# Gate and up products of the last layer by seven block products in place of eight

## What is computed

```
g = jnp.einsum('bsh,ehf->ebsf', x, w_gate)      # h = 256, f = 1024, 8 experts
u = jnp.einsum('bsh,ehf->ebsf', x, w_up)
h = jax.nn.silu(g) * u
expert_out = jnp.einsum('ebsf,efh->ebsh', h, w_down)
cw = router_probs * gate_weights                # two softmaxes over the 8 experts
cw = cw / (jnp.sum(cw, axis=-1, keepdims=True) + 1e-09)
out = jnp.einsum('ebsh,bse->bsh', expert_out, cw)
```

## Time and profile before

| | |
|---|---|
| three runs, median | 1771.9 us |
| profiled execution, span from the first to the last instruction | 1770.5 us |
| PE busy, of the span | 93% |
| first gate or up matmul of the last layer | 701.3 us |
| last matmul | 1765.2 us |
| clock granted to PE, 750 to 1650 us | 1.00 of full speed |
| DVE, ACT, POOL busy in 880 to 1010 us (one expert is 130.6 us) | 70.1, 24.4, 15.2 us of 130 |

### The profile page before, as it was taken

The page is one execution under the profiler, slowest core; times in us unless marked ns, Lnnn a source line. Parts: engine busy times, 40 slices in busy tenths (PEclk is TensorE's granted clock), DMA queues, the critical chain, the costliest instruction groups (busy, mean ns, idle before and its releaser), DMA issues.

```text
span 1770.5 us, 24802 instructions
## 1 busy us (share of the span) xinstructions
PE 1646.7 (93%) x8306; PEld 1355.8 (77%) x8306; DVE 1043.8 (59%) x2102; ACT 478.5 (27%) x845; POOL 459.8 (26%) x297
## 2 busy tenths in 40 slices
PE   6999987689966888999999999999999999999998
PEld 5896663388864777788888888888888888888887
DVE  6666778556656786554555554554655544645654
ACT  4455332134332455312212212212112112112111
POOL 2552257688526612100201201101101102102000
PEclk9998998899987998899999999999999999999999
DMA  6994022278643201000200200200101101101001
GB/s 204 265 315 185 24 71 87 84 242 272 209 133 121 80 2 36 26 36 19 78 1 19 77 0 18 77 0 28 66 0 36 59 0 36 59 0 36 24 12 36
DMA packets 73309, 136.09 MB, mean 77 GB/s; under 512 B 8464, under 2 KB 52048, under 8 KB 72080
## 3 DMA queue, kind: packets, MB, share of 16 engines
q1 hardware_dynamic: 39392, 92.76, 16.0%
q10 hardware_dynamic: 27696, 25.51, 4.5%
q0 software_dynamic: 6144, 16.79, 3.0%
HBM read 90.93 MB, written 44.11 MB: 76 GB/s over the span
## 4 chain that ended last, share of the span: by engine, by line
PE 78%; POOL 6%; issue 5%; DMA 5%; DVE 4%; ACT 1%; SPq 0%; POOLq 0%; DVEq 0%; ACTq 0%
PE ps L2369 40%; PE ps L2392 19%; PE ps L2188 4%; DMA slots_in<-xn,idS 3%; PE ps L2207 2%; POOL slots_in L1805 2%; POOL yg L1844 2%; PE ps L1880 2%; PE ps L2168 1%; PE ps L2285 1%; DMA yg<-slots_out,idG 1%; DMA x<-in_x 1%; PE ps L1950 1%; PE ps L1949 1%; PE ps L2263 1%
## 5 line engine op out<-in xcount | busy, mean ns | idle before, releaser
L1273 DVE TENSOR_TENSOR hF<-sg,ps 128x512 f32<-128x512 f32 x256 | 175.9, 687 | 460.4 <-ACT sg L1456 460.4
L2369 PE MATMUL ps<-xTH,wH 128*128 128x512 f32 x1024 | 401.1, 392 | 4.8 <-DVE hF L1273 4.8
L2369 PE MATMUL ps<-xTH,wL 128*128 128x512 f32 x1024 | 400.1, 391 | 0.0
L2369 PE MATMUL ps<-xTL,wH 128*128 128x512 f32 x1024 | 400.1, 391 | 0.0
L1456 ACT ACTIVATE sg<-ps 128x512 f32<-128x512 f32 x264 | 157.7, 598 | 865.0 <-PE ps L2369 842.4
L1861 POOL TENSOR_TENSOR wL<-wS,wH 128x1536 fp32r<-128x1536 f32 x32 | 120.4, 3764 | 867.8 <-ACT wH L1615 867.8
L2369 PEld LDWEIGHTS ps<-xTH,wH 128*128 128x128 f32 x1024 | 193.3, 189 | 45.0 <-issue 5.2
L2369 PEld LDWEIGHTS ps<-xTL,wH 128*128 128x128 f32 x1024 | 193.2, 189 | 40.5
L2369 PEld LDWEIGHTS ps<-xTH,wL 128*128 128x128 f32 x1024 | 193.4, 189 | 39.9
L2392 PE MATMUL ps<-hH,wH 128*128 128x512 f32 x496 | 193.0, 389 | 0.0
L2392 PE MATMUL ps<-hH,wL 128*128 128x512 f32 x496 | 192.9, 389 | 0.0
(11 more groups left out here) (412 smaller groups left out, 2552.1 us busy)
## 6 DMA issues: line engine op xcount, KB each, us to landing
wS<-in_w SPq DMA_DIRECT2D x32, 768.0 KB, 4.7
slots_in<-eS SPq DMA_DIRECT2D x16, 768.0 KB, 12.1
eS<-in_wr SPq DMA_DIRECT2D x32, 384.0 KB, 4.0
xl<-slots_in ACTq DMA_DIRECT2D x48, 256.0 KB, 3.8
slots_out<-yo ACTq DMA_DIRECT2D x48, 256.0 KB, 3.0
cwB<-expert_weights SPq DMA_DIRECT2D x8, 1024.0 KB, 4.7
k_parts<-parts SPq DMA_DIRECT2D x8, 512.0 KB, 5.2
q_parts<-parts SPq DMA_DIRECT2D x8, 512.0 KB, 3.9
```

Source lines behind the costliest of these rows:

```text
L1273: dve.tensor_tensor(hF[:, b, :], sg[:, b, :], ps[:, 2 + b, :], ALU.mult).then_inc(mul_done, 1)
L2369: last = pe.matmul(ps[:, 2 * half + b, :], w[:, col:col + P], v[:, k, g * 512:(g + 1) * 512], start=q == 0, stop=q == 5)
```

## The change

Tokens are taken in pairs of groups (even, odd), the contraction in two halves of 128 features, a chunk's hidden features in two tiles. That makes gate and up each a 2 x 2 by 2 x 2 block product; it is computed with seven block products P1 to P7 in place of eight, with sums that are shared (Winograd's form).

- POOL makes three sums of weight blocks per chunk and half product in the raw chunk (`chunk_sums`, four instructions of 128 x 256), so that a chunk grows from 1536 to 2304 columns (`CW`). ACT copies high parts in three pieces of 768 columns, POOL subtracts in six pieces of 384.
- DVE makes three sums of token blocks per pair (`tF3`, split into `tH`, `tL`), and stores the odd group's first half as the difference to the even one (`last_odd`); the router products get a third term for that.
- A "superstep" is a chunk by a pair, and does what four steps did: 14 products of 3 matmuls, and 4 down units of 6 matmuls, which belong to the superstep before. There are 8 supersteps per expert, 64 in all.
- Partial sums are taken out of PSUM and built up in SBUF: ACT copies banks 0 and 1 three times per superstep (`snapshot`, to `gU1`, `gU2`, `gU3`), DVE adds banks 2 and 3 to the copies (`half_sum`). PE goes on adding to banks 0 and 1 after each copy. Three of four hidden blocks are products of two SBUF tiles, one has its up half in bank 1.
- ACT, not DVE, makes the high part of the hidden block (`high_of`).
- All four chunks have their own buffers; a chunk is loaded again when the last unit that used it is done (`unit_done`), two and a half supersteps ahead of its use. `cwB` is loaded in halves.
- The first chunk is loaded when block A3's product with `dcw` is done, and its sums, high and low parts come within block B3. The first router products move behind down product 1 of block B3. In the first superstep there are no down units yet.

The core of the diff (the loops on PE, DVE, ACT and POOL; `...` marks what is left out):

```diff
+                for q, (w, v) in enumerate(((cH[c], high), (cL[c], high), (cH[c], low))):
+                    last = pe.matmul(ps[:, bank, :], w[:, col:col + P], v, start=name in ("P1", "P2", "P5") and q == 0,
+                                     stop=q == 2, skip_group_check=True)
+                last.then_inc(product_done, 1)
...
+                both("P1")
...
+                units(0)
...
+                both("P6")
...
+                both("P2")
+                both("P7")
...
+                units(1)
+                both("P5")
+                units(2)
+                both("P4")
+                both("P3")
+                units(3)
...
+                if name in ("P6", "P7", "P4"):
+                    pe.wait_ge(snap_done, e * 48 + (6 * s + {"P6": 1, "P7": 3, "P4": 5}[name] + half))
+                if name in ("P5", "P3"):
+                    pe.wait_ge(half_summed, e * 48 + (6 * s + {"P5": 1, "P3": 3}[name] + half))
...
+                dve.tensor_tensor(eF[:, b, :], gate, up, ALU.mult).then_inc(hidden_made, 1)
...
+                dve.tensor_tensor(eL[:, b, :], eF[:, b, :], f32(eH[:, b, :]), ALU.subtract).then_inc(block_low, 1)
...
+                dve.tensor_tensor(to[:, :], ps[:, 2 + half, :], to[:, :], ALU.add).then_inc(half_summed, 1)
...
+                act.activation(to[:, :], ps[:, half, :], ACT.Identity).then_inc(snap_done, 1)
...
+                pool.tensor_tensor(extra(1), block(0, 0), block(0, 1), ALU.subtract).then_inc(block_summed, 1)
+                pool.wait_ge(block_summed, done + 1)
+                pool.tensor_tensor(block(0, 1), block(0, 1), block(1, 1), ALU.add).then_inc(block_summed, 1)
+                pool.wait_ge(block_summed, done + 2)
+                pool.tensor_tensor(extra(0), block(0, 1), block(0, 0), ALU.subtract).then_inc(block_summed, 1)
+                pool.wait_ge(block_summed, done + 3)
+                pool.tensor_tensor(extra(2), block(1, 0), extra(0), ALU.subtract).then_inc(chunk_summed, 1)
...
-                pool.tensor_tensor(chunk_low(c), wS[:, 1 - c % 2, :], f32(chunk_high(c)), ALU.subtract).then_inc(w_low, 1)
+                for part in range(6):
+                    cols_ = slice(part * CW // 6, (part + 1) * CW // 6)
+                    pool.wait_ge(chunk_high, e * 12 + (3 * c + part // 2 + 1))
+                    last = pool.tensor_tensor(cL[c][:, cols_], cR[c][:, cols_], f32(cH[c][:, cols_]), ALU.subtract)
```

More of the change, by code:

```diff
@@ new lines, in build @@
+        for c, (high, low) in enumerate(((start["dcw"], start["dcw"] + 4 * CW), (start["wS"], start["wS"] + 4 * CW),
+                                         (start["wS"] + 8 * CW, start["wS"] + 12 * CW), (start["sc0"], start["dcw"] + 8 * CW))):
+            cH.append(at(f"cH{c}", [P, CW], F32R, high))
+            cL.append(at(f"cL{c}", [P, CW], F32R, low))
+            cR.append(at(f"cR{c}", [P, CW], F32, low))
+        assert end["cL2"] <= end["wL"] and end["cH3"] <= end["selm"] and end["cL0"] == start["cL3"]
@@ new lines, in build @@
+        gU2 = [at(f"gU2{h}", [P, 512], F32, end["tL0"] + 2048 * h) for h in range(2)]
+        cwT = at("cwT", [P, P], F32, end["gU21"])
+        assert end["cwT"] <= end["vext"] and start["tH1"] >= end["vext"] and end["tL1"] <= end["eS"]
+        eH = at("eH", [P, 4, 512], F32R, start["sg"])
+        eF = at("eF", [P, 4, 512], F32, end["eH"])
+        eL = at("eL", [P, 4, 512], F32R, end["eH"])
+        gU1 = [at(f"gU1{h}", [P, 512], F32, end["eF"] + 2048 * h) for h in range(2)]
+        assert end["gU11"] <= end["tF"]
@@ L421, in slot_rows, with copies, snapshots @@
             return yg[:, i, :, :] if i < 4 else ya[:, 4 * i - 8:4 * i - 4, :]
[L423 to L429, removed]
+        def copies(kind, g):
+            return sum(1 if k == "L" and n % 2 else 2 for k, n in TURNS[:TURNS.index((kind, g))]) + 8
+        def snapshots(half):
+            return gU1[half], gU2[half], gU3[half]
         def blocks(t, slot, plain):
@@ new lines, in mixed, with add_out @@
+            def mixed(e, s, part, j):
+                if s // 4 == 0 and isinstance(e, int) and e == 0:
+                    return
+                of = (e, 0) if s // 4 else (e - 1, 1)
+                (weigh, add)[part](*of, j)
+            def add_out(k):
+                g = (2, 3, 0, 1)[k]
+                for t in range(2):
+                    dve.wait_ge(out_turned, k + 1)
+                    rows = x[:, 4 * g + 2 * t:4 * g + 2 * t + 2, :]
+                    dve.tensor_tensor(rows, ps[:, 2 + t, :].rearrange("p (n d) -> p n d", n=2), rows, ALU.add).then_inc(out_ready, 1)
@@ L1340, in _ @@
+            def body(e, first=False, last=False):
+                for s in range(STEPS):
+                    superstep(e, s, first, last)
             body(0, first=True)
@@ L1674, in _ @@
             turned("B", 3)
-            act.wait_ge(down_done, 8 * (U_L1 - 1))
-            chunk_split(0, 0)
+            sums_of(0)
+            for part in range(3):
+                high(0, 0, part)
             ffn_silu("B", 3, 0)
@@ L1680, in _ @@
             ffn_silu("B", 3, 1)
-            chunk_split(0, 1)
+            for part in range(3):
+                high(0, 1, part)
             ffn_silu("B", 3, 2)
@@ L1713, in _ @@
+            def expert(e, first=False, last=False):
+                for s in range(STEPS):
+                    superstep(e, s, first, last)
             expert(0, first=True)
-            with act.Fori(1, E1 - 1) as e:
+            expert(1)
+            with act.Fori(2, E1 - 1) as e:
                 expert(e)
             expert(E1 - 1, last=True)
+            high_of(E1 - 1, STEPS - 1, 3)
         @block.gpsimd
@@ L2432, in _ @@
+            def expert(e, first=False, last=False):
+                for s in range(STEPS):
+                    superstep(e, s, first, last)
+            pe.wait_ge(silu_done, FIRST + 32)
             expert(0, first=True)
-            with pe.Fori(1, E1 - 1) as e:
+            expert(1)
+            with pe.Fori(2, E1 - 1) as e:
                 expert(e)
             expert(E1 - 1, last=True)
+            for b in range(4):
+                unit(E1 - 1, STEPS - 1, b, True)
 def constants(np):
```

734 lines of the change are left out of this document (430 added, 304 removed).

## The result

| | before | after |
|---|---|---|
| median of four executions, one chip | 1772.2 us | 1725.4 us |
| median of nine and five executions, another chip (`after_again`) | 1771.1 us | 1721.5 us |
| span of the profiled execution | 1770.5 us | 1727.2 us (`after_again` 1721.4) |

The ratio is 0.9729, 95% interval 0.9706 to 0.9752; on the other chip 0.9715 (0.9698 to 0.9731). The change saves 47 to 50 us. The forecast was 1691.7 us with a range up to 1720: the sign is right, the gain is 60% of the one forecast, and the time lies above the range.

A forecast was written before the change was run, and what follows sets the result against it. PE was taken as the bound. First product at 704, first four supersteps 68.8, 60 x 14.96 = 897.6, then turnings, last units, POOL 2 and the end gave 1690.3 us, as median 1691.7; range 1676 to 1720.

The forecast's parts named there:

- Matmuls removed: PE in the last layer: 4224 matmuls instead of 4608, the 384 removed worth 87.0 us at 0.2267 us each.
- the long stretch: From the fifth superstep to the end of the last matmul: forecast 912.3 us, with supersteps of 14.96 us.
- DVE against POOL: DVE instructions on two SBUF tiles slowed beside POOL's pieces in supersteps with a chunk: 2 us, bounds 0 to 28.
- the half sum that I followed: DVE's half sum for P2, where a pair's sum closes: made at about 6.8 us, P5 due at 8.15, 1.4 left.
- The first four supersteps: Start of the last layer: 16, 15.5, 21 and 16.3 us, together 68.8, bounds 63 and 76.
- The first product: P1 of the first superstep, behind block B3 and L2's normalising: starts at 704 us, bounds 698 and 712.
- Semaphores on PE: 18 signals per superstep on PE, where four steps had 8: cost 0.
- Waits inside a superstep: PE's waits for copies, half sums and hidden products: each has 1.1 us or more in hand; stall without POOL 0.
- The clock stayed at 1.00: Rival: late copies make PE pause and the clock fall, 136 us if once per superstep, 1828 us; chance 5%.
- DVE did not become the bound: Rival: DVE's 8 instructions each wait a full POOL piece, 70 us over 28 supersteps, 1760 us; chance 8%.
- waits did not cost PE a fixed price: Rival: each of 18 waits per superstep on PE costs 0.08 us, 92 us in all, 1784 us; chance 3%.

The follow-up runs named there:

- after_again: The changed kernel as it is, run once more on another chip: 1721.5 us, ratio 0.9715.
- e1_offsets: Changed kernel with cH3 and token sums tH, tL moved in SBUF, so all tiles PE reads in the last layer start at 128 modulo 512 bytes: 1710.7 us.
- e7_little_pool: e1_offsets, but from the second expert on no chunk loads and no POOL sums or low parts, only two one-column instructions per chunk: 1698.9 us.
- e3_before_signals: Kernel before, with 12 more semaphore signals and 16 more waits on PE per four steps: 1773.6 us, ratio 0.9999.
- e2_before_moved: Kernel before, with 128 bytes left free ahead of xTH, so weights and tokens of chunks 2 and 3 start differently modulo 256: 1788.5 us, ratio 1.0072.
- e8_half_k: e1_offsets with the token sums tH, tL at 384 modulo 512 bytes instead of 128: 1711.0 us, ratio 0.9662.

## Why the prediction was wrong

- **Matmuls removed, 0.2267 us each: the count holds, the price does not.** This is the step that failed. I read the pitch from the earlier trace rows and carried it to a kernel with other tiles. The row holds where weights and moving tile start at the same offset modulo 256 bytes, as all tiles of the kernel before do; `cH3`, `tH` and `tL` do not. The prediction took one price for every matmul, without a bound and without a word on the new operands. Cost: 12.4 us (`e1_offsets`), of 19.8 in the long stretch; with the offsets mended the kernel takes 1710.7 us, inside the range. With POOL away as well, `e7_little_pool` shows the forecast 14.96 us in every superstep.
- **DVE against POOL: right in mechanism, mis-sized.** 2 us were taken from bounds of 0 to 28; 10.4 us were measured at full pace (`e7_little_pool`), part of them hidden in the changed kernel behind the slow matmuls. POOL's pieces take 1.02 us instead of 0.9 and its sums 0.73 to 1.2 instead of 0.6, so it works 10 us per chunk, not 8. And the late instruction was not only the half sum that I followed: the hidden product for P1's second half was a second one, and the dearer.
- **The first four supersteps: 76.2 and 78.0 us instead of 68.8, at or beyond the upper bound.** The third superstep was the long one, as forecast, but took 29.1 us, not 21: DVE makes the second pair's sums ahead of a hidden product, PE waits 3.71 us, and works at 0.43 us per matmul behind it and the router. The first superstep took 13.2 us, not 16, the second 17.4, not 15.5: that these two misses partly cancel is luck.
- **The first product: 704 forecast, 713.5 and 705.6.** Of the 9.5 us, 6.4 stand ahead of block B3's first matmul (681.9 against 675.5 in the profile of before) and are the difference between executions. Of the other 3, DVE has 1: its added instructions beside POOL took about 10 us, not 5, and L2's normalising starts 12.6 us behind that matmul, not 11.5. The rest is no fault of the sum: in `after_again` DVE is as late, and P1 comes 29.0 us behind block B3's first matmul, where 28.5 were forecast. The first profile has 31.6, since more of PE's matmuls on that way, the router's thin ones among them, ran at a granted clock of 0.50.
- **Semaphores on PE, 0: right** (`e3_before_signals`). **Waits inside a superstep: right**, the fourth to eighth superstep having no stall at all, and none of the eight with POOL away (`e7_little_pool`).
- **Rivals.** The clock stayed at 1.00 from 780 us on, DVE did not become the bound, waits did not cost PE a fixed price. None of the three was the cause. The range left the pitch itself without a bound, and its other terms had to be near their upper ends to reach 1720.

## What to carry over

A distance between matmuls that is read from a trace holds for the tiles of that trace: when a change brings new operands, compare where weights and moving tiles start (here modulo 256 bytes) before multiplying, and lay them out alike. Work given to POOL is paid for by DVE (here 0.69 us became up to 1.50 beside pieces of 1.02, and 3.73 in the earlier trace rows beside an instruction of 3.49), so look for every instruction of DVE on which PE waits within that stretch, not only the tightest. Where PE has just been made faster, stalls that it used to hide come up: after each gain read the waits anew.

## What the runs showed of the hardware

- PE's pitch for 128 x 512 fp32r matmuls at a granted clock of 1.00 is 0.2267 us when weights and moving tile start at the same offset modulo 256 bytes, and 0.231 to 0.235 on average over a group when they differ, for differences of 64 and 128 bytes (`after`, `e1_offsets`, `e2_before_moved`, `e8_half_k`); the matmuls behind such ones are slowed too. Why is not shown.
- Even DVE instructions of four columns grow beside POOL, by the trace of the changed kernel: 0.17 us alone, 0.57 for one that starts within one of POOL's sums. It ends with that sum (692.41 and 692.39), as the ones before and behind it do that start within a sum; those that start in the gap between two sums take 0.16.

```profile
691.66 0.73 POOL L2030 TENSOR_TENSOR cR<-cR 128x256 f32<-128x256 f32 x1
691.84 0.57 DVE L1101 TENSOR_TENSOR u<-u,vA 128x4 f32<-128x4 f32 x1
...
719.43 0.17 DVE L1101 TENSOR_TENSOR u<-u,vA 128x4 f32<-128x4 f32 x1
```
